# Row sums of the attention's softmax: four TensorE transposes and a VectorE reduction in place of products with a column of ones

## The reference, cut to what matters

```
q, k, v = x @ (codes * scales) + bias
scores  = einsum("bqhd,bkhd->bhqk", q, k) / sqrt(128)
attn    = softmax(scores, axis=-1)
out     = einsum("bhqk,bkhd->bqhd", attn, v) @ wo + bo
```

## Time and profile before

| | |
|---|---|
| median of 3 runs | 2954.38 us (2952.43 to 2956.91) |
| the profiled execution, its own time | 2951.71 us |
| its span, from the first to the last instruction | 2949.6 us |
| PE busy / DVE busy / ACT busy / POOL busy | 2749.2 / 2004.3 / 1429.6 / 1786.8 us |
| row-sum products L1279 | first at 681.0 us, last at 2639.2 us |

### The profile page before, as it was taken

How to read it: one execution, slowest core, us unless ns; L and a number is a source line. 1 busy time by engine, 2 the same in 40 slices (tenths; PEclk the granted TensorE clock), 3 DMA queues, 4 the chain that set the end, 5 groups by cost and what they waited for, 6 DMA issues and landing times. The chain is left out here.

```text
span 2949.6 us, 32974 instructions
## 1 busy us (share of the span) xinstructions
PE 2749.2 (93%) x11130; PEld 1904.6 (65%) x11131; DVE 2004.3 (68%) x2508; ACT 1429.6 (48%) x1749; POOL 1786.8 (61%) x1086
## 2 busy tenths in 40 slices
PE   5886799889999999999999999999999999977995
PEld 2232677667677777777777767776777777647663
DVE  4478543468778788787887787787787787863211
ACT  1201322146656665665666566566656656641121
POOL 0022230038878787896888788688788878874002
PEclk9888699989999999999999999999999999987997
DMA  2000100010000000000000000000000000006012
GB/s 63 0 0 0 50 0 0 21 25 4 20 4 8 13 8 7 8 18 4 8 16 5 8 17 8 4 8 17 7 8 4 8 1 4 1 24 240 17 46 77
DMA packets 57727, 57.81 MB, mean 20 GB/s; under 512 B 8336, under 2 KB 52624, under 8 KB 57584
## 3 DMA queue, kind: packets, MB, share of 16 engines
q1 hardware_dynamic: 54944, 48.75, 5.6%
q0 software_dynamic: 2640, 7.21, 0.7%
HBM read 45.72 MB, written 10.22 MB: 19 GB/s over the span
## 5 line engine op out<-in xcount | busy, mean ns | idle before, releaser
L1339 ACT ACTIVATE at_prob<-at_psum_s 128x1024 f32<-128x1024 f32 x512 | 522.8, 1021 | 670.0 <-PE at_psum_s L578 644.1
L1264 PE MATMUL at_psum_o<-at_prob,at_v 128*128 128x512 f32 x1536 | 707.5, 596 | 0.0
L1398 DVE TENSOR_TENSOR at_prob<-at_prob,at_psum_m 128x1024 f32<-128x1024 f32 x512 | 605.2, 1213 | 48.5 <-PE at_psum_m L1252 48.5
L1411 DVE TENSOR_TENSOR at_top<-at_psum_s,at_top 128x1024 f32<-128x1024 f32 x448 | 547.2, 1221 | 92.0 <-ACT at_prob L1339 82.0
L1529 POOL TENSOR_TENSOR at_acc<-at_acc,at_prob 128x1024 f32<-128x1024 f32 x192 | 459.0, 2391 | 235.4 <-ACT at_prob L1345 231.1
L1345 ACT ACTIVATE at_prob<-at_prob 128x1024 f32<-128x1024 f32 x512 | 538.5, 1052 | 24.0 <-DVE at_prob L1398 23.7
L1533 POOL TENSOR_TENSOR at_acc<-at_acc,at_prob 128x1024 f32<-128x1024 f32 x192 | 461.2, 2402 | 0.0
L1264 PEld LDWEIGHTS at_psum_o<-at_prob,at_v 128*128 128x128 f32 x1536 | 282.7, 190 | 258.5 <-issue 244.6
L1546 POOL TENSOR_TENSOR at_p_lo<-at_prob,at_p_hi 128x512 fp32r<-128x512 f32 x256 | 347.5, 1357 | 149.8 <-ACT at_p_hi L1352 139.4
L576 PE MATMUL at_psum_s<-at_q_hi,at_k_hi 128*128 128x512 f32 x1024 | 406.7, 397 | 5.0 <-DVE at_k_lo L1390 5.0
L577 PE MATMUL at_psum_s<-at_q_lo,at_k_hi 128*128 128x512 f32 x1024 | 400.9, 392 | 0.0
(11 more groups left out here) (324 smaller groups left out, 4606.9 us busy)
## 6 DMA issues: line engine op xcount, KB each, us to landing
ef_gate_up<-in_ef_gate_up SPq DMA_DIRECT2D x8, 1024.0 KB
ef_down<-in_ef_down SPq DMA_DIRECT2D x8, 512.0 KB
ef_rows_in<-ef_zeros SPq DMA_DIRECT2D x23, 128.0 KB, 1.8
ef_rows<-ef_rows_in SPq DMA_DIRECT2D x23, 128.0 KB, 2.0
ef_rows_out<-ef_result POOLq DMA_DIRECT2D x23, 128.0 KB, 2.0
x_tok<-in_L_attn_x SPq DMA_DIRECT2D x1, 2048.0 KB, 8.1
lf_w<-in_L_ffn_W SPq DMA_DIRECT2D x2, 1024.0 KB, 6.6
at_codes<-in_at_wq_codes SPq DMA_DIRECT2D x16, 128.0 KB, 2.1
```

The costliest lines, as they stand in the source:

```text
L1264: nc.tensor.matmul(psum_o[:], v[:, c, t, half], prob[u % 2][:, c * KPC + t, :], start=(c == 0 and t == 0), stop=False)
L1339: nc.scalar.activation(prob[u % 2][:, c * KPC + 2 * half:c * KPC + 2 * half + 2, :], psum_s[:, 2 * half:2 * half + 2, :], ACT.Copy).then_i ...
L1398: nc.vector.tensor_tensor(part, part, psum_m[:].unsqueeze(1).to_broadcast([P, 2, BT]), ALU.subtract).then_inc(shifted, 1)
L1411: nc.vector.tensor_tensor(top2[:], part, top2[:], ALU.max).then_inc(maxed, 1)
```

## The change

The column `ones` is no longer made. `sum_rows` turns the four tiles of `acc` into a whole bank, in the way of `turn_top`; `invert_sums` adds 128 columns for each query with a `tensor_reduce` out of PSUM into `rsum`, releases the bank with it, waits for its own result, and takes the reciprocal in place. `add` waits on a new semaphore, `inverted`, instead of on the release of the bank. Three initial waits count one constant less.

```diff
-        ones = alloc("at_ones", [P, 2])
...
-                nc.gpsimd.memset(ones[:], 1.0).then_inc(constants, 1)
...
+            inverted = semaphore("at_inverted")
...
                         for t in range(TPB):
-                            last = nc.tensor.matmul(bank(key)[:, t:t + 1], acc[:, bass.ts(t, P)], ones[:, 0:1],
-                                                    start=True, stop=True)
+                            last = nc.tensor.transpose(bank(key)[:, bass.ts(t, P)], acc[:, bass.ts(t, P)], ident[:])
                         last.then_inc(w_ready, 1)
...
-                    pe.wait_ge(constants, 3)
+                    pe.wait_ge(constants, 2)
...
                     def invert_sums(u):
                         key = ("sum", u)
                         dve.wait_ge(w_ready, jobs[key] + 1)
-                        nc.vector.reciprocal(rsum[:, u % 2, :], bank(key)[:, 0:TPB]).then_inc(w_free, 1)
+                        nc.vector.tensor_reduce(rsum[:, u % 2, :], bank(key).rearrange("p (t k) -> p t k", t=TPB), AX.X,
+                                                ALU.add).then_inc(w_free, 1)
+                        dve.wait_ge(w_free, jobs[key] + 1)
+                        nc.vector.reciprocal(rsum[:, u % 2, :], rsum[:, u % 2, :]).then_inc(inverted, 1)
...
                     def add(u, half):
                         key = ("out", u, half)
                         dve.wait_ge(w_ready, jobs[key] + 1)
-                        dve.wait_ge(w_free, jobs["sum", u] + 1)
+                        dve.wait_ge(inverted, u + 1)
```

More of the change, by code:

```diff
@@ L1359, in out_hi @@
                         nc.scalar.activation(oT_hi[:], psum_o[:], ACT.Copy).then_inc(oT_hi_ready, 1)
-                    act.wait_ge(constants, 3)
+                    act.wait_ge(constants, 2)
                     project_hi(0, 0, 0)
@@ L1474, in take_v @@
                         made.then_inc(w_free, 1)
-                    dve.wait_ge(constants, 3)
+                    dve.wait_ge(constants, 2)
                     project_lo(0, 0, 0)
```

## The result

The changed kernel takes 2939.91 us in the median of 5 runs (2934.23 to 2943.92), the kernel before 2956.7 us (2952.43 to 2958.83). The ratio is 0.9943, with a 95% interval of 0.9926 to 0.9961: faster by 0.57%, or 16.8 us by the medians. Forecast were 24.8 us and 2929.6 us, and a range up to 2938.0. The sign was right; the time lies 1.9 us above the range. The two intervals overlap, so a part of the miss is spread; the profiles tell which part. The base moved too: the forecast stood on 2954.4 us from three runs, and five runs of the kernel before give 2956.7. Taken as a saving, the range began at 2954.4 - 2938.0 = 16.4 us, and 16.8 were measured.

A forecast was written before the change was run, and what follows sets the result against it. TensorE, busy throughout the attention loop, was taken as the bound. 28.8 us saved, less 4.2 given back, plus 0.2 at the tail made 24.8: from 2954.4 to 2929.6 us, range 2923 to 2938 for 8 in 10.

The forecast's parts named there:

- Price of the exchange on TensorE: At each sum between scores and weigh, transposes replace products of ones: 3.30 to 2.85 us, saving 0.45 a unit, 28.8 over 64.
- VectorE's addition and its cover: Reduction and waits before add cost VectorE 0.74 us a unit, hidden by gaps of 1.48 and 1.16 us in 57 units.
- The rival in which VectorE takes over: Reduction delays add, shift, exponentials and weigh by 0.74 us a unit against 0.45 gained: +18.6 us, 2973.0 us; chance 3%.
- The give-back: In six GpSimd stretches TensorE waits for the low part, losing 0.45 us plus 0.25 through late shifts each: 4.2 us.
- a late `add`: In the unit after v's projection, add runs 0.5 us behind TensorE's new pace; half, 0.25 us, was counted per stretch.
- The sum on the loop: Saving of 0.45 us in each of 64 units, 28.8 us, less 4.2 us given back, taken as the loop's whole.
- the bound of 0.38 us a unit: Lower bound of the exchange's saving, read only to the next start after the sum: at least 24.3 us over 64 units.
- The ends of the range: 8 in 10: 2923 us (all kept, less 2 us of single-run spread) to 2938 us (nearly the more-given-back rival).
- The tail: Last unit's sum falls from 1.70 to 0.85 us at the lower clock, 0.3 may come back before add; +0.2 us counted.
- The rival drawn from the Trainium skill: Clock falls behind the transposes: weigh's six products run at 1.2 GHz, +144 us less 29, 3069 us; chance 2%.
- `tensor_reduce` as the dear operation: VectorE's reduction in invert_sums: skill calls it slowest; prediction read 681 ns against 173 as agreeing, but under TensorE's cover.

The follow-up runs named there:

- e9: Kernel before with out_lo first and v's split later, plus four spare transposes of the accumulator ahead of the products of ones; loop 2018.8 us, median 2968.51 us.
- e1: Changed kernel without the reduction: one column a tile, plus one, replaces reduction and reciprocal; loop 1973.1 us against 1973.0, median 2930.95 us.
- e2: Kernel before plus a spare reduction of the bank and a wait for it, ahead of the reciprocal; loop 1994.1 us against 1993.0, median 2951.75 us.
- e5: Changed kernel with out_lo ahead of the shift in units after v's projection and GpSimd's v split four steps later; loop 1968.7 us, ratio 0.9916.
- e6: Kernel before with out_lo ahead of the shift in units after v's projection and GpSimd's v split four steps later; loop 1993.0 us, ratio 1.0008.
- e8: Changed kernel with out_lo first, v's split later, and sum_rows issued behind weigh instead of ahead; loop 1970.9 us against 1968.7, median 2936.08 us.
- the second's: The unaltered changed kernel measured once more beside other kernels; 2934.68 us, ratio 0.9916, loop 1973.3 us.

## Why the prediction was wrong, point by point

* **Price of the exchange on TensorE: right at the place.** 2.85 against 3.30 us, 0.45 a unit; e9 gives 0.43 for the transposes by themselves.
* **VectorE's addition and its cover: right.** 0.68 + 0.04 + 0.18 us in place of 0.17, under a gap that kept 0.75 us in the ordinary unit. e1 and e2 show that the reduction moves the loop by nothing measurable after its first eighth. The rival in which VectorE takes over is refuted.
* **The give-back: size right by luck, one of its two mechanisms wrong.** I had 6 x (0.45 + 0.25) = 4.2 us. Freeing both holders returns 4.3 us (e5). Of that, GpSimd's stretch is as forecast in kind, not in size. In place of the 0.25 us through a late `add`, TensorE lost the unit's whole saving earlier, at `weigh`, which waits for `out_lo`; the row that looked like an ordinary start stood 0.10 us behind `out_lo`'s end already. With the whole 0.43 us lost there in seven units, less was left for GpSimd to take: about 0.19 us in each of six stretches instead of 0.45, or 7 x 0.43 + 6 x 0.19 = 4.2. Forecast were 2.7 us for GpSimd and 1.5 for VectorE; it was 1.1 and 3.0, and the two misses cancel.
* **The sum on the loop: the step that failed.** It took 64 times the local saving less the give-back as the whole. But with the products of ones gone, other products of TensorE ran a little slower, 62 x 0.45 - 24.3 = 3.6 us over the loop with both holders removed. Counted by starts in e6 and e5, as the mean of the ordinary units from u = 10 on, the step with the sum (c = 2) is 0.437 us shorter, while the two steps ahead of it (c = 0 and 1) are 0.013 and 0.017 us longer and the one behind 0.004: 0.40 us a unit are left of 0.45. The two units in eight around v's projection keep only 0.32 and 0.36. No term of the sum and no bound stood for it: the bound of 0.38 us a unit was meant for something else, and covers it only by chance (62 x 0.38 = 23.6). e1 excludes the reduction as its source, e9 the transposes as such, e8 the place of the sum ahead of `weigh`. What stays open is why the steps ahead of a sum take longer when the products of ones are missing.
* **The ends of the range: the second failure.** I took 2 us for the spread around the loop. But the loop's start moved from 602.5 to 618.1 us over eleven profiles. TensorE's idle time ahead of it is 85 to 87 us in all of them; what differs is how long it ran at 1.2 GHz (granted clock up to 600 us: 0.88 in e9, which starts first, 0.86 in e8, which starts last). The time behind the loop moved from 344.5 (e1: 2928.9 - 2584.4) to 356.7 us (e5: 2932.0 - 2575.3), with the wait in the routed network that some profiles have and with the clock. The first measurement's 2939.9 and the second's 2934.7 us belong to loops of equal length. In the profiles, the saving fell 3.7 us short of the forecast in the loop (20.0 against 27.9 - 4.2) and 3.8 us short behind it (-2.7 against 1.1). Only the loop's 20 us, and 1.3 us of the last sums, are the change.
* **The tail: right.** The last sum takes 2618.10 - 2617.36 = 0.74 us after, against 1.70 in the earlier trace rows; `add` still waits 0.38 us.

```profile
2617.36 1.08 PE L1278 MATMUL at_psum_w<-ident,at_acc 128*128 128x128 f32 x4 [2.78 <-POOL at_acc L1539]
...
2618.10 0.56 PE L576 MATMUL at_psum_w<-at_wo_hi,at_oT_hi 128*128 128x256 f32 x1
...
2619.77 0.88 DVE L1445 SCALAR_TENSOR_TENSOR x_tok<-at_psum_w,at_rsum,x_tok 128x256 f32<-128x256 f32 x2 [0.38 <-PE at_psum_w L578]
```

* **The clock in the loop stayed at 1.00 with twelve transposes a unit**, in the window from 600 to 2610 us of the kernel after. The rival drawn from the Trainium skill, "TensorE: Matmul & The Clock Gate", Part 4, did not come about beside dense products; its statement on transposes alone is not tested here.

```profile
600.00:2610.00 2010.00, 1995.66 (x8425) 1413.50 (x8424) 1654.75 (x1881) 1261.08 (x1472) 1624.69 (x941) 1.00 0.04 9
```

* **A reading that does not hold: `tensor_reduce` as the dear operation.** The Trainium skill, "VectorE: DVE Perf Modes", Rules for kernel authors, calls it "the slowest DVE op". The prediction saw that borne out by 681 ns against 173, but these are 512 columns against 4. A `tensor_tensor` of 512 columns out of PSUM, `out_lo`, takes the same 0.68 us, so the trace does not show the reduction to be slower. Nothing in the forecast hung on it, and under TensorE's cover the reduction cost nothing.

## What to carry to other kernels

Where an engine is busy throughout, look for the places at which another one arrives just in time, also those that the list of waits calls "issue": read the code's waits at each start that follows another engine's end by 0.1 us. Such holders can stand in series, as here: removing one returned 0.5 or 1.0 us, removing both 4.3. Check a move of work against the shared banks too (e8). And compare kernels by the length of the changed stretch in the profile before comparing whole times, when the parts around it change their clock from run to run by more than the effect.

## What the runs showed of the hardware that was not expected

A product with one moving column is not cheap when its operands are plain fp32: eight such instructions (four products) take 0.81 us to the next start, and the pair behind starts another 0.08 us late, twice the 0.43 us of four full transposes of 128 columns. Yet taking them out of TensorE's stream made other products slower by 3.6 us in 1969, mostly in the two steps ahead of each sum, and putting four transposes beside them did not (a step of `score` is 12 products, 48 a unit).
